# Column sums of the adjacency: from reductions on VectorE to accumulating transfers on GpSimd's queue

## The chip, the cores and the metric

The kernel runs on one core of a Trainium2 chip. The metric is the device time of one launch in microseconds (us), lower is better. The engines are named as in the profile: PE is TensorE (PEld its weight loads), DVE is VectorE, ACT is ScalarE, POOL is GpSimd, SP is SyncE. SP and POOL here only issue transfers; "SPq" is SP's queue.

## The reference, cut to what matters

`x` is [3327, 256] and `adj` is [3327, 3327], all float32. Two graph layers follow each other. The first one needs, beside the row sums of the adjacency, its column sums:

```python
S = S + jnp.eye(n)
Rf = S / jnp.clip(S.sum(axis=1, keepdims=True), 1e-12)
Rb = S / jnp.clip(S.sum(axis=0), 1e-12)[:, None]      # column sums
for s in range(2):                                    # STEPS
    A = _adj_from_feats(Xa, W1, W2, W3)               # softmax over the nucleus (0.9) of each row's logits
    Xf, Xb, Xa = Rf @ Xf, Rb @ Xb, A @ Xa
    Z = Z + (Xf @ U1[s] + Xb @ U2[s] + Xa @ U3[s])
```

The column sums are first used after step one (s = 0), when its products are scaled. The second layer is a masked attention, which the change doesn't touch.

## The kernel before, in words

The 3327 nodes are padded to 3328 = 26 tiles (`T`) of `P` = 128 rows. `step(0)` ("step one", from about 72 us to 1103 us of the span) runs 26 tiles; `between` multiplies by the weights; `step(1)` repeats the work for step two; then comes the second layer. In each step every engine has its own instruction stream, written out by hand, and semaphores order them. The names in the trace carry `s_` for tensors of a step.

A tile t of step one goes through these stages, which are spread over the engines and over three tiles in time:

- PE `make_logits` (L916) computes the tile's 7 chunks of logits into two banks in turn, ACT `store_logits` (L1043) copies each out of its bank.
- DVE `row_max` (L1235) takes the maximum of the row and sends `max_ready` (L1241). ACT `exponentials` (L1050) waits for it, and then runs `guess` and two `probe`s (L1083, L1087, and small instructions to L1101), which end with `searched_early`.
- DVE `start_search` (L1273) waits for `searched_early`; `bisect` runs three times (L1315, late = 3), `threshold` (L1357 to L1383) finds the limit and sends `tau_ready`, `count_needed` (L1388 to L1405) follows.
- ACT `count_ties` (L1128, waits for `tau_ready`) and `lift` (L1134); DVE `settle` (L1410 on) and `keep` (L1428), which sends `kept_ready`.
- PE `turn` (L942) transposes the kept weights, ACT copies them (L1150), PE `multiply` (L952) multiplies; ACT `read_attended` (L1163) and SP store the result.

Beside this, PE `spread` (L928) multiplies each tile of the adjacency. SP's `load_half` (L856) fetches tile t in two halves of [128, 1664] into `adj`; there are NA = 2 pairs of buffers, so tile t+2 is loaded when tile t is used up. `sum_columns(t, h)` (L1433) on DVE also reads each half: it adds up 13 groups of 128 elements into `col_part`. At the end of the step one more DVE reduction (L1525) adds the 26 tiles' parts into `col_inv`.

The order of DVE's stream for tile t is: start_search(t), bisect(t, 0), settle(t-1), row_max(t+1), keep(t-1), bisect(t, 1), bisect(t, 2), sum_columns(t, 0), threshold(t), sum_columns(t, 1), count_needed(t). That of ACT is: store_logits(t+1) chunks 0 and 1, count_ties(t-1), store_logits(t+1) the rest, lift(t-1), exponentials(t+1), guess(t+1), the copies of tile t-1 among the two probes of t+1, read_attended(t-1).

Of the kernel before, what the change touches and what calls it, by code (L numbers as in the profile page):

```python
# [9 lines left out]
ALU = mybir.AluOpType  # L10
ACT = mybir.ActivationFunctionType
AX = mybir.AxisListType

P = 128
# [530 lines left out]
def program(nc, s, x, adjb, adjr, ident_d, W1, W2, W3, U1, U2, U3, gamma, beta, Wks, Wqs, Wvs, WvT, Wo, out):  # L545
    N, T, NP, D, DA, KT = s.N, s.T, s.NP, s.D, s.DA, s.KT
# [10 lines left out]
    with whole, ctx:  # L557
# [206 lines left out]
        def step(number, both):  # L764
# [3 lines left out]
            with ExitStack() as c:  # L768
                def sbt(name, shape, dt=F32):
                    return c.enter_context(nc.sbuf_tensor(tag + name, shape, dt))  # L770

                if first_step:
                    width = SW
                    col_part = sbt("col_part", [P, T, T])
                    spread_out = [sbt(f"spread_out{i}", [P, SW]) for i in range(2)]
                    att_out = [sbt(f"att_out{i}", [P, D]) for i in range(2)]
                else:
                    width = 2 * D
                    z_row = [sbt(f"z_row{i}", [P, D]) for i in range(4)]
                    fold = sbt("fold", [P, DA])  # L780
                    key_sum = sbt("key_sum", [P, 1])
# [41 lines left out]
                         "turned_stored", "attended_groups", "spread_read", "att_read", "setup", "constants_set", "dve",  # L823
                         "act", "low_ready"]
                if first_step:
                    names += ["adj2_loaded", "adj3_loaded", "adj_summed", "spread_stored0", "spread_stored1",
                              "att_stored0", "att_stored1"]
                else:
                    names += ["adj_checked", "guessed", "keys_summed", "keys_folded", "keys_ready", "z_added"]
                    names += [f"z_loaded{i}" for i in range(4)] + [f"z_stored{i}" for i in range(4)]  # L830
# [10 lines left out]
                def half(t, h):  # L841
                    return adj[t % NA * 2 + h][:, :]

                def half_loaded(eng, t, h):
                    eng.wait_ge(sem[f"adj{t % NA * 2 + h}_loaded"], 16 * (t // NA + 1))

                @block.sync
                def _(sp):
                    def load_half(t, h):
                        if t >= NA:  # L850
                            sp.wait_ge(sem[f"adj{h}_used"], t - NA + 1)
                            if first_step:
                                sp.wait_ge(sem["adj_summed"], 2 * (t - NA) + h + 1)
                            else:
                                sp.wait_ge(sem["adj_checked"], 2 * (t - NA) + h + 1)
                        sp.dma_start(half(t, h), adjb[t, :, h * HALF * P:(h + 1) * HALF * P]  # L856
                                     ).then_inc(sem[f"adj{t % NA * 2 + h}_loaded"], 16)

                    def load_z(t):
                        sp.dma_start(z_row[t % 4][:, :], z_d[t, :, :]).then_inc(sem[f"z_loaded{t % 4}"], 16)  # L860

                    def store_z(t):
                        sp.wait_ge(sem["z_added"], t + 1)
                        sp.dma_start(z_d[t, :, :], z_row[t % 4][:, :]).then_inc(sem[f"z_stored{t % 4}"], 16)

                    def store_attended(t):
                        sp.wait_ge(sem["att_read"], t + 1)
                        sp.dma_start(attended_d[t, :, :], att_out[t % 2][:, :]
                                     ).then_inc(sem[f"att_stored{t % 2}"], 16)

                    for t in range(NA):
                        load_half(t, 0)
                        load_half(t, 1)
                    if not first_step:
                        load_z(0)
                        load_z(1)
                    for t in range(T):
                        if not first_step and t > 1:
                            store_z(t - 2)
                        if not first_step and t + 2 < T:  # L880
                            if t >= 2:
                                sp.wait_ge(sem[f"z_stored{(t + 2) % 4}"], 16 * ((t + 2) // 4))
                            load_z(t + 2)
                        if t + NA < T:
                            load_half(t + NA, 0)
                        if first_step:
                            sp.wait_ge(sem["spread_read"], t + 1)
                            sp.dma_start(spread_d[t, :, :], spread_out[t % 2][:, :]
                                         ).then_inc(sem[f"spread_stored{t % 2}"], 16)
                        if t + NA < T:  # L890
                            load_half(t + NA, 1)
                        if first_step and t > 0:
                            store_attended(t - 1)
                    if first_step:
                        store_attended(T - 1)
                        for i in range(2):
                            sp.wait_ge(sem[f"spread_stored{i}"], 16 * (T // 2))
                            sp.wait_ge(sem[f"att_stored{i}"], 16 * (T // 2))
                    else:
                        store_z(T - 2)  # L900
                        store_z(T - 1)
                        for i in range(4):
                            sp.wait_ge(sem[f"z_stored{i}"], 16 * ((T - i + 3) // 4))
# [125 lines left out]
                def _(act):  # L1029
# [145 lines left out]
                    for t in range(T + 1):  # L1175
# [33 lines left out]
                        else:  # L1209
# [16 lines left out]
                            else:  # L1226
                                turned(3, 4, 5, 6)

                @block.vector
                def _(dve):  # L1230
                    chain = Steps(dve, sem["dve"])
# [196 lines left out]
                        dve.scalar_tensor_tensor(kept, kept, col(t, "sharetau"), expd[t % NE][:, :],  # L1428
                                                 ALU.add, ALU.min).then_inc(sem["kept_ready"], 1)

                    def sum_columns(t, h):
                        half_loaded(dve, t, h)
                        dve.tensor_reduce(col_part[:, t, h * HALF:(h + 1) * HALF],  # L1433
                                          half(t, h).rearrange("q (j r) -> q j r", r=P), AX.X, ALU.add
                                          ).then_inc(sem["adj_summed"], 1)

                    def add_spread(t):
                        z = z_row[t % 4][:, :]
                        dve.wait_ge(sem[f"z_loaded{t % 4}"], 16 * (t // 4 + 1))
# [40 lines left out]
                    for t in range(T):  # L1480
                        following, previous = t + 1 < T, t > 0
                        start_search(t)
                        if first_step:
                            bisect(t, 0)
                            if previous:
                                settle(t - 1)
                            if following:
                                row_max(t + 1)
                            if previous:
                                keep(t - 1)  # L1490
                            for k in range(1, late):
                                bisect(t, k)
                            sum_columns(t, 0)
                            threshold(t)
                            sum_columns(t, 1)
                            count_needed(t)
                        else:
                            if previous:
                                settle(t - 1)
                            bisect(t, 0)  # L1500
                            if previous:
                                add_spread(t - 1)
                                keep(t - 1)
                            bisect(t, 1)
                            if following:
                                row_max(t + 1)
                            if t > 1:
                                add_attended(t - 2)
                            bisect(t, 2)
                            if following:  # L1510
                                guess(t + 1)
                            for k in range(3, late):
                                bisect(t, k)
                            threshold(t)
                            count_needed(t)
# [5 lines left out]
                    if not first_step:  # L1521
                        add_attended(T - 1)
                    if first_step:
                        dve.wait_ge(sem["adj_summed"], 2 * T)
                        chain.did(dve.tensor_reduce(col_inv[:, :], col_part[:, :, :].rearrange("q t j -> q j t"),  # L1525
                                                    AX.X, ALU.add))
                        chain.wait()
                        chain.did(dve.tensor_scalar(col_inv[:, :], col_inv[:, :], 1.0, 1e-12, ALU.add, ALU.max))
                        chain.wait()
                        chain.did(dve.reciprocal(col_inv[:, :], col_inv[:, :]))  # L1530
                        chain.wait()
# [257 lines left out]
```

## Time and profile before

| | us |
|---|---|
| median of 3 runs (2746.53 to 2748.87) | 2747.1 |
| the profiled execution, its time | 2744.11 |
| its span, first to last instruction | 2742.1 |
| DVE busy | 2326.4 |
| PE busy | 2266.8 |
| ACT busy | 1911.6 |
| POOL busy | 0.2 |

The difference between the profiled execution's time and its span, 2.0 us, is what lies around the instructions. Busy shares are averages over stages that have different limits; for a change in one stage the rows of that stage are read.

### The profile page before, as it was taken

To read this page: it belongs to the slowest core of one execution; us is meant where nothing else is said; L and a number is where in the kernel's file an instruction comes from. 1 tells how busy PE (TensorE), PEld (TensorE's weight loads), DVE (VectorE), ACT (ScalarE), POOL (GpSimd) and SP (SyncE) were. 2 spreads that over 40 slices of the span, in tenths; PEclk is the share of its full clock that TensorE was granted. 3 is DMA by queue.
4 is the path that set the end of the run, shared out by engine and by line. 5 is a ranking of instruction groups with operands and counts; after the bars stand their busy time and mean duration, and the time that the engine had idled before them with its cause. 6 is when DMAs were issued, how large, how long until landed. Compare 5 with 4: busy or idle time off the path is not lost. (4 is left out here: it accounts for less than half of the span.)

```text
span 2742.1 us, 25827 instructions
## 1 busy us (share of the span) xinstructions
PE 2266.8 (83%) x8302; PEld 1449.3 (53%) x8302; DVE 2326.4 (85%) x4827; ACT 1911.6 (70%) x2579; POOL 0.2 (0%) x4
## 2 busy tenths in 40 slices
PE   5588888888888887899489889898898988989736
PEld 2366666666666666444145545455454554545425
DVE  3499999999999998344699999999999999999825
ACT  3788898888898885233767767677676776767313
POOL 0000000000000000000000000000000000000000
PEclk9699999999999998998689999999999999999868
DMA  1111111111111110311001111111111111111031
GB/s 54 64 45 56 58 58 44 58 44 58 58 57 44 52 51 7 104 58 60 27 25 46 42 33 45 38 46 42 35 40 41 46 42 33 44 40 44 17 122 50
DMA packets 63309, 132.06 MB, mean 48 GB/s; under 512 B 10306, under 2 KB 49857, under 8 KB 63169
## 3 DMA queue, kind: packets, MB, share of 16 engines
q1 hardware_dynamic: 60704, 128.76, 14.9%
q10 hardware_dynamic: 2464, 1.61, 0.2%
q8 instruction: 67, 1.10, 0.2%
q14 instruction: 74, 0.60, 0.1%
HBM read 113.29 MB, written 17.05 MB: 48 GB/s over the span
## 5 line engine op out<-in xcount | busy, mean ns | idle before, releaser
L1315 DVE SCALAR_TENSOR_TENSOR s_junk<-s_logits,s_small,s_expd 128x3327 uint8<-128x3327 f32 x208 | 766.2, 3684 | 7.2
L928 PE MATMUL bank<-both,s_adj 128*128 128x512 f32 x1352 | 646.0, 629 | 0.0
L952 PE MATMUL bank<-h_aug,s_attT 128*128 128x256 f32 x2704 | 626.6, 380 | 20.3 <-ACT s_attT L1150 20.3
L952 PEld LDWEIGHTS bank<-h_aug,s_attT 128*128 128x128 f32 x2704 | 501.9, 190 | 126.4 <-issue 35.9
L928 PEld LDWEIGHTS bank<-both,s_adj 128*128 128x128 f32 x1352 | 270.1, 205 | 294.8 <-issue 292.0
L916 PE MATMUL bank<-KTr,QT 64*128 64x512 f32 (+1 forms) x728 | 275.7, 646 | 142.0 <-ACT s_logits L1043 141.3
L942 PE MATMUL bank<-ident,s_logits 128*128 128x128 f32 x1352 | 216.8, 303 | 194.7 <-DVE s_logits L1428 194.7
L1150 ACT ACTIVATE s_attT<-bank 128x512 f32<-128x512 f32 (+1 forms) x364 | 193.7, 563 | 204.8 <-PE bank L942 182.2
L928 PE MATMUL bank<-h_aug,s_adj 128*128 128x257 f32 x1352 | 333.6, 398 | 2.9 <-ACT s_spread_out L1157 2.9
L1083 ACT ACTIVATE s_junk<-s_expd,s_small 128x3327 int8<-128x3327 f32 x104 | 319.1, 3069 | 1.8
L1087 ACT ACTIVATE s_junk<-s_expd,s_small 128x3327 int8<-128x3327 f32 x104 | 319.4, 3072 | 1.0
L942 PEld LDWEIGHTS bank<-ident,s_logits 128*128 128x128 f32 x1352 | 180.9, 157 | 257.4 <-DVE s_logits L1428 215.9
L928 PEld LDWEIGHTS bank<-h_aug,s_adj 128*128 128x128 f32 x1352 | 257.5, 197 | 86.5 <-issue 47.7
L1050 ACT ACTIVATE s_expd<-s_logits,s_small 128x3327 f32<-128x3327 f32 x52 | 159.6, 3070 | 160.5 <-DVE s_small L1241 86.7
L1043 ACT ACTIVATE s_logits<-bank 128x512 f32<-128x512 f32 (+1 forms) x364 | 188.9, 564 | 99.8 <-PE bank L916 99.7
L916 PEld LDWEIGHTS bank<-KTr,QT 64*128 64x128 f32 x728 | 97.7, 194 | 293.7 <-ACT s_logits L1043 274.8
L1364 DVE MAX8 s_small<-s_logits 128x8 f32<-128x416 f32 (+1 forms) x416 | 209.9, 577 | 0.0
L1235 DVE TENSOR_REDUCE s_small<-s_logits 128x1 f32<-128x3327 f32 x52 | 188.2, 3619 | 24.0 <-ACT s_logits L1043 22.2
L1428 DVE SCALAR_TENSOR_TENSOR s_logits<-s_logits,s_small,s_expd 128x3328 f32<-128x3328 f32 x52 | 191.2, 3676 | 1.9 <-ACT s_logits L1134 1.9
L1357 DVE SCALAR_TENSOR_TENSOR s_logits<-s_logits,s_small,s_expd 128x3327 f32<-128x3327 f32 x52 | 191.3, 3679 | 0.9
L1128 ACT ACTIVATE s_junk<-s_logits,s_small 128x3327 int8<-128x3327 f32 x52 | 159.7, 3072 | 43.6 <-DVE s_small L1383 43.6
L1134 ACT ACTIVATE s_logits<-s_expd,s_small 128x3327 f32<-128x3327 f32 x52 | 159.3, 3064 | 0.9
(213 smaller groups left out, 1878.1 us busy)
## 6 DMA issues: line engine op xcount, KB each, us to landing
s_adj<-adj_turned SPq DMA_DIRECT2D x104, 832.0 KB, 4.6
spread<-s_spread_out SPq DMA_DIRECT2D x26, 128.5 KB, 5.0
m_spread_in<-spread SPq DMA_DIRECT2D x26, 128.5 KB, 2.2
attended<-s_att_out SPq DMA_DIRECT2D x26, 128.0 KB, 4.6
m_att_in<-attended SPq DMA_DIRECT2D x26, 128.0 KB, 2.2
z<-m_z_out SPq DMA_DIRECT2D x26, 128.0 KB, 1.7
s_z_row<-z SPq DMA_DIRECT2D x26, 128.0 KB, 2.0
z<-s_z_row SPq DMA_DIRECT2D x26, 128.0 KB, 1.7
```

Of the source, the lines that this page charges most:

```text
L916: pe.matmul(LB[i % 2][:, 0:w], QT[r:r + DA, bass.ts(t, P)], keys_of(n, w), start=True, stop=True).then_inc(sem["logits_done"], 1)
L928: done = pe.matmul(SX[:, 0:width], half(t, h)[:, bass.ts(jj, P)], rows_of(j), start=(j == 0), stop=(j == T - 1))
L942: last = pe.transpose(TB[i % 4][:, bass.ts(b, P)], kept[:, bass.ts(g + b, P)], ident[:, :])
L952: last = pe.matmul(AB[:, 0:D], attT[i % 4][:, b, :], h_aug[:, g + b, 0:D], start=(g + b == 0), stop=(g + b == T - 1))
L1043: act.activation(logits[t % 3][:, at:at + w], LB[i % 2][:, 0:w], ACT.Copy).then_inc(sem["logits_stored"], 1)
L1083: chain.did(act.activation(junk2[:, 0:N], e, ACT.Relu, bias=at, scale=-0.5, accum_out=col(t, "tail")))
L1087: chain.did(act.activation(junk2[:, 0:N], e, ACT.Sign, bias=at, scale=-0.5, accum_out=col(t, "side")))
L1150: act.activation(attT[i % 4][:, 0:w, :], TB[i % 4][:, 0:w * P].rearrange("q (b r) -> q b r", r=P), ACT.Relu).then_inc(sem["turned_stored"], 1)
L1315: chain.did(dve.scalar_tensor_tensor(junk[:, 0:N], logits[t % 3][:, 0:N], col(t, "cand"), expd[t % NE][:, 0:N], ALU.is_gt, ALU.mult, accum ...
L1357: chain.did(dve.scalar_tensor_tensor(me[:, 0:N], logits[t % 3][:, 0:N], col(t, "cand"), expd[t % NE][:, 0:N], ALU.is_le, ALU.mult, accum_o ...
L1364: chain.did(dve.max(winners(t)[:, 8 * n:8 * n + 8], me[:, at:min(at + NP // SEGMENTS, N)]))
L1428: dve.scalar_tensor_tensor(kept, kept, col(t, "sharetau"), expd[t % NE][:, :], ALU.add, ALU.min).then_inc(sem["kept_ready"], 1)
```

## The change

`sum_columns` and its `col_part` are gone. POOL gets a stream of its own in step one: for each tile it issues two transfers of [128, 1664] from `adjb` (named `adj_turned` in the trace, the same array that SP loads) into a new array `adj_total` (two halves). The first pair overwrites, the other 25 pairs add to what is there (`accum_op`). Before each pair POOL waits for the pair before it. At the end DVE waits for all 52 transfers and reduces `adj_total` to `col_inv`, in two instructions of 13 groups each. SP's loads of step one no longer wait for the sums.

```diff
-                    col_part = sbt("col_part", [P, T, T])
+                    adj_total = [sbt(f"adj_total{i}", [P, HALF * P]) for i in range(2)]
...
                         if t >= NA:
                             sp.wait_ge(sem[f"adj{h}_used"], t - NA + 1)
-                            if first_step:
-                                sp.wait_ge(sem["adj_summed"], 2 * (t - NA) + h + 1)
-                            else:
+                            if not first_step:
                                 sp.wait_ge(sem["adj_checked"], 2 * (t - NA) + h + 1)
...
+                @block.gpsimd
+                def _(pool):
+                    def add_adjacency(t):
+                        if t > 0:
+                            pool.wait_ge(sem["adj_added"], 32 * t)
+                        for h in range(2):
+                            part = adjb[t, :, h * HALF * P:(h + 1) * HALF * P]
+                            if t == 0:
+                                pool.dma_start(adj_total[h][:, :], part).then_inc(sem["adj_added"], 16)
+                            else:
+                                pool.dma_start(adj_total[h][:, :], part, accum_op=ALU.add).then_inc(sem["adj_added"], 16)
+
+                    if first_step:
+                        for t in range(T):
+                            add_adjacency(t)
...
-                    def sum_columns(t, h):
-                        half_loaded(dve, t, h)
-                        dve.tensor_reduce(col_part[:, t, h * HALF:(h + 1) * HALF],
-                                          half(t, h).rearrange("q (j r) -> q j r", r=P), AX.X, ALU.add
-                                          ).then_inc(sem["adj_summed"], 1)
...
-                            sum_columns(t, 0)
                             threshold(t)
-                            sum_columns(t, 1)
                             count_needed(t)
...
-                        dve.wait_ge(sem["adj_summed"], 2 * T)
-                        chain.did(dve.tensor_reduce(col_inv[:, :], col_part[:, :, :].rearrange("q t j -> q j t"),
-                                                    AX.X, ALU.add))
+                        dve.wait_ge(sem["adj_added"], 32 * T)
+                        for h in range(2):
+                            chain.did(dve.tensor_reduce(col_inv[:, h * HALF:(h + 1) * HALF],
+                                                        adj_total[h][:, :].rearrange("q (j r) -> q j r", r=P),
+                                                        AX.X, ALU.add))
```

The first place is DVE's stream in step one, at tile t = 1: the end of bisect(1, 2), threshold(1) and the start of count_needed(1). Before:

```order
L1346 TENSOR_SCALAR s0_small1<-s0_small1 128x1
L1349 SCALAR_TENSOR_TENSOR s0_small1<-s0_small1 128x1
L1433 TENSOR_REDUCE s0_col_part<-s0_adj2 128x13
L1357 SCALAR_TENSOR_TENSOR s0_logits1,s0_small1<-s0_logits1,s0_small1,s0_expd1 128x3327
L1361 TENSOR_TENSOR s0_small1<-s0_small1 128x1
L1364 MAX s0_small1<-s0_logits1 128x8 x8
```

The same place of the change (line numbers are 14 higher):

```order
L1360 TENSOR_SCALAR s0_small1<-s0_small1 128x1
L1363 SCALAR_TENSOR_TENSOR s0_small1<-s0_small1 128x1
L1371 SCALAR_TENSOR_TENSOR s0_logits1,s0_small1<-s0_logits1,s0_small1,s0_expd1 128x3327
L1375 TENSOR_TENSOR s0_small1<-s0_small1 128x1
L1378 MAX s0_small1<-s0_logits1 128x8 x8
```

The reduction of the adjacency half stood ahead of threshold's first pass, and is gone; the second one stood between L1383 and L1388 and is gone in the same way. All else keeps its order.

The second place is POOL's queue in step one, which had nothing before. It begins so (`s_adj_total` is the new array):

```order
L1235 DMA s_adj_total<-adj_turned 128x1664 x2
L1237 DMA s_adj_total<-adj_turned 128x1664 [waits s0_adj_added]
L1237 DMA s_adj_total<-adj_turned 128x1664
L1237 DMA s_adj_total<-adj_turned 128x1664 [waits s0_adj_added]
L1237 DMA s_adj_total<-adj_turned 128x1664
```

26 pairs follow each other, each behind the landing of the one before, and with no wait on any other engine.

The third place is the end of DVE's stream in step one. Before:

```order
L1422 RECIPROCAL s_small<-s_small 128x1 [waits s0_dve]
L1428 SCALAR_TENSOR_TENSOR s_logits<-s_logits,s_small,s_expd 128x3328 [waits s0_lifted,s0_dve]
L1525 TENSOR_REDUCE col_inv<-s_col_part 128x26 [waits s0_adj_summed]
L1528 TENSOR_SCALAR col_inv<-col_inv 128x26 [waits s0_dve]
L1530 RECIPROCAL col_inv<-col_inv 128x26 [waits s0_dve]
```

And of the change:

```order
L1436 RECIPROCAL s_small<-s_small 128x1 [waits s0_dve]
L1442 SCALAR_TENSOR_TENSOR s_logits<-s_logits,s_small,s_expd 128x3328 [waits s0_lifted,s0_dve]
L1532 TENSOR_REDUCE col_inv<-s_adj_total 128x13 [waits s0_adj_added]
L1532 TENSOR_REDUCE col_inv<-s_adj_total 128x13
L1536 TENSOR_SCALAR col_inv<-col_inv 128x26 [waits s0_dve]
L1538 RECIPROCAL col_inv<-col_inv 128x26 [waits s0_dve]
```

The last reduction now waits for the last pair of transfers, and there are two of it.

## Rows read from the trace of the kernel before

**Rows 1.** The page: span, and busy time by engine.

```profile
span 2742.1 us, 25827 instructions
PE 2266.8 (83%) x8302; PEld 1449.3 (53%) x8302; DVE 2326.4 (85%) x4827; ACT 1911.6 (70%) x2579; POOL 0.2 (0%) x4
```

**Rows 2.** A window in step one: us, busy by engine, clock share, DMA share, GB/s.

```profile
400.00:600.00 200.00, 170.12 (x758) 127.37 (x758) 193.22 (x349) 174.33 (x237) 0.00 (x0) 0.98 0.18 55
```

**Rows 3.** Timeline of DVE: start us, us, line, operation; one tile.

```profile
487.11 3.62 DVE L1235 TENSOR_REDUCE s_small<-s_logits 128x1 f32<-128x3327 f32 x1
...
502.94 1.89 DVE L1433 TENSOR_REDUCE s_col_part<-s_adj 128x13 f32<-128x1664 f32 x1
504.74 3.67 DVE L1357 SCALAR_TENSOR_TENSOR s_logits<-s_logits,s_small,s_expd 128x3327 f32<-128x3327 f32 x1
...
515.33 1.88 DVE L1433 TENSOR_REDUCE s_col_part<-s_adj 128x13 f32<-128x1664 f32 x1
...
518.72 0.15 DVE L1273 TENSOR_SCALAR s_small<-s_small 128x1 f32<-128x1 f32 x1
...
524.73 3.62 DVE L1235 TENSOR_REDUCE s_small<-s_logits 128x1 f32<-128x3327 f32 x1
```

**Rows 4.** The column sums on DVE in all of step one.

```profile
L1433 DVE TENSOR_REDUCE s_col_part<-s_adj x52: 1874/1882/1890, 126.5 to 1076.1; 128x13 f32<-128x1664 f32 x52
```

**Rows 5.** Timeline of ACT, the same tile; idle before and its releaser in brackets.

```profile
490.95 3.07 ACT L1050 ACTIVATE s_expd<-s_logits,s_small 128x3327 f32<-128x3327 f32 x1 [3.35 <-DVE s_small L1241]
...
514.04 0.39 ACT L1101 ACTIVATE s_small<-s_small 128x1 f32<-128x1 f32 x1
...
521.89 0.39 ACT L1043 ACTIVATE s_logits<-bank 128x256 f32<-128x256 f32 x1 [0.30 <-PE bank L916]
522.17 3.06 ACT L1134 ACTIVATE s_logits<-s_expd,s_small 128x3327 f32<-128x3327 f32 x1
```

**Rows 6.** Timeline of PE, the same tile.

```profile
511.15 1.13 PE L916 MATMUL bank<-KTr,QT 64*128 64x512 f32 x4
...
521.79 7.22 PE L928 MATMUL bank<-h_aug,s_adj 128*128 128x257 f32 x32
532.19 1.53 PE L942 MATMUL bank<-ident,s_logits 128*128 128x128 f32 x12 [3.18 <-DVE s_logits L1428]
```

**Rows 7.** Timeline of DVE: the row maxima of tiles 2 and 25.

```profile
148.25 3.62 DVE L1235 TENSOR_REDUCE s_small<-s_logits 128x1 f32<-128x3327 f32 x1
...
1013.96 3.62 DVE L1235 TENSOR_REDUCE s_small<-s_logits 128x1 f32<-128x3327 f32 x1
```

**Rows 8.** Timeline of ACT: the last logits of tile 2 copied.

```profile
147.63 0.38 ACT L1043 ACTIVATE s_logits<-bank 128x256 f32<-128x256 f32 x1 [0.30 <-PE bank L916]
```

**Rows 9.** Timeline of DVE, then ACT: the end of step one.

```profile
1076.10 1.88 DVE L1433 TENSOR_REDUCE s_col_part<-s_adj 128x13 f32<-128x1664 f32 x1
...
1082.58 3.68 DVE L1428 SCALAR_TENSOR_TENSOR s_logits<-s_logits,s_small,s_expd 128x3328 f32<-128x3328 f32 x1 [1.85 <-ACT s_logits L1134]
1086.18 1.44 DVE L1525 TENSOR_REDUCE col_inv<-s_col_part 128x26 f32<-128x676 f32 x1
...
1102.77 0.47 ACT L1163 ACTIVATE s_att_out<-bank,s_small 128x256 f32<-128x256 f32 x1 [3.94 <-PE bank L952]
```

**Rows 10.** Transfers of step one: issues, KB each, median us to landing.

```profile
s_adj<-adj_turned SPq DMA_DIRECT2D x52, 832.0 KB, 4.6
spread<-s_spread_out SPq DMA_DIRECT2D x26, 128.5 KB, 5.0
```

**Rows 11.** Timeline of SP's queue: first loads of step one; a tile's first half.

```profile
72.48 56.27 SPq L856 DMA_DIRECT2D s_adj<-adj_turned  x5
...
504.92 0.33 SPq L856 DMA_DIRECT2D s_adj<-adj_turned  x1
```

**Rows 12.** Timeline of PE: the start of step one; the first use of that half.

```profile
105.08 2.56 PE L916 MATMUL bank<-KTr,QT 64*128 64x512 f32 x4 [18.71 <-ACT s_logits L1043]
...
549.83 2.01 PE L928 MATMUL bank<-h_aug,s_adj 128*128 128x257 f32 x8
```

More of the change, by code:

```diff
@@ L825, in step @@
                 if first_step:
-                    names += ["adj2_loaded", "adj3_loaded", "adj_summed", "spread_stored0", "spread_stored1",
+                    names += ["adj2_loaded", "adj3_loaded", "adj_added", "spread_stored0", "spread_stored1",
                               "att_stored0", "att_stored1"]
```

## The prediction

> **What bounds the kernel now.** The page first: DVE is busy for 2326.4 of 2742.1 us, more than PE and ACT [rows 1]. That is a mean over stages, so the windows inside step one come next: of 200 us DVE works 193.22, ACT 174.33, PE 170.12, and the transfer engines are busy for 0.18 of the time [rows 2]. So DVE bounds step one. The timeline of one tile gives the size: from one row maximum to the next (L1235, 487.11 to 524.73) it is 37.62 us, with no idle time shown ahead of any of DVE's instructions [rows 3]. Then I asked how near the others are. ACT has one long wait in a tile, 3.35 us for DVE's maximum (L1050) [rows 5]; PE waits 3.18 us for DVE's `keep` (L942) [rows 6]. Both are waits for DVE; they shrink when DVE gets faster, and how far is what decides here.
>
> **What the change removes.** 52 reductions L1433 of 1.88 us [rows 4]. They overlap the instruction behind them a little: the first one of a tile starts at 502.94 and the next instruction at 504.74 [rows 3], which is 1.80; the second one is as long. So a tile has 3.60 us less of DVE's stream, and DVE alone would need 37.62 - 3.60 = 34.02 us.
>
> **What then is late.** Follow the longest loop that DVE's sums are not part of. Call R the start of a row maximum. ACT's exponentials (L1050) start at R + 3.84 (490.95 - 487.11). From there ACT runs without another long wait to the end of the next tile's last logits copy, at 521.89 + 0.39 = 522.28, which is 31.33 us later [rows 3, 5]. The small waits inside are for PE's banks, which PE in turn gets back from ACT; they belong to the loop. The row maximum of the next tile needs that copy. The hand-over I put at 0.10: between L1235's end (490.73) and L1050's start (490.95) lie 0.22 us, with one small instruction and one hand-over in them. The loop is 3.84 + 31.33 + 0.10 = 35.27 us. It is longer than DVE's 34.02, so the period becomes 35.27, and a tile gains 2.35 us, not 3.60. DVE then waits 1.2 us ahead of L1235 in every tile.
>
> I went through the other waits with R as the origin. `searched_early` is there at 514.04 + 0.39, R + 27.3; DVE asks for it at 518.72 - 487.11 - 3.60 = R + 28.0 (no wait, 0.7 us to spare) [rows 3, 5]. `lift` ends at 522.17 + 3.06 = 525.23; `keep` would start at 522.38 + 3.7 = 526.1 (0.9 to spare) [rows 5]. PE ends its spread at 521.79 + 7.22 = 529.01, R + 41.9, and `keep`, which ends two instructions of 3.7 us behind the start of a row maximum, is ready at R + 35.27 + 7.4 = R + 42.7 (0.8 to spare); its next logits start at 511.15, ACT copies them after 514.43 [rows 5, 6]. Nothing else ends later than the ACT loop, but all margins are under 1 us.
>
> **The sum.** Tile 2 is the first with the full pattern: its maximum starts at 148.25, its logits are there at 148.01, so it can start at 148.11 [rows 7, 8]: 0.14 us. To the maximum of tile 25 at 1013.96 it is 865.7 us for 23 periods; 23 x 35.27 = 811.2, so 54.5. After it there is no further row maximum: DVE's last stretch loses both sums of tile 24 (3.60) and the first of tile 25 (1.80). The second one of tile 25 lies behind `tau_ready`, and DVE waited for ACT's lift there anyway (1.85 us) [rows 9]: nothing. Together 0.1 + 54.5 + 5.4 = 60.0 us.
>
> The new last reductions are two like L1433, 2 x 1.8 us for 1.44 before. Behind `keep` PE and ACT work until 1102.77 + 0.47 = 1103.24, 17 us after L1525 began [rows 9]; the reductions end 13 us before that. Cost nothing; if that cover were gone, 2.2 us.
>
> SP's loads lose a wait. They were not late: a half issued at 504.92 lands in 4.6 us and is first read at 549.83, 45 us after issue [rows 10 to 12]. Gain nothing.
>
> **What it adds: 52 accumulating transfers.** No row of before shows one. A round is the pair of a tile, 2 x 0.85 MB, each round behind the landing of the last. From below: a plain load of the same shape lands in 4.6 us [rows 10], so a pair takes at least that. From above, the slowest transfers of the step: 128.5 KB in 5.0 us [rows 10], which at that rate is 65 us for 1664 KB. An accumulate reads two places and writes one and is otherwise nearest in shape to the plain load (same source, same 128 rows of 1664 floats), so I take two reads in turn for each half: 4 x 4.6 = 18 us for a pair. Then 26 rounds end at about 72 + 26 x 18 = 540 us, in the middle of step one, and DVE's last wait is over long before.
>
> The point from which it counts: step one would end at 1103.2 - 60 = 1043.2; DVE needs some 4.2 us behind the last landing (3.6 for the two reductions and 0.6, an estimate, for the small ones behind), and the first load of the step is issued at 72.48 [rows 11]. So rounds may take (1043.2 - 4.2 - 72.5) / 26 = 37.2 us before they cost anything, and at (1103.2 - 4.2 - 72.5) / 26 = 39.5 us the whole gain is used up. 37 us is twice my estimate and eight times the lower bound.
>
> A rule beside it: the Trainium skill (Collectives: The Full Stack, The bandwidth ceiling) holds that adding on the way costs nothing by itself, and that a reducing transfer runs at half the rate of a copy, since each piece needs two source reads. No row of before can show that. By it a pair takes 9 to 18 us, and the sum stays the same.
>
> The new transfers share the transfer engines with SP's. These are busy for 0.18 now [rows 2]. If the accumulates fill them, a load takes three times as long, 14 us, against 45 us of room. At the start of the step ACT holds PE for 18.71 us [rows 12], so late first halves cost nothing either.
>
> **The rivals.**
>
> *A. The transfers are too slow* (the other side). One mechanism: the chain of 26 rounds, not DVE, ends step one, and DVE waits at L1532 of the changed kernel. The step ends at 72.5 + 26r + 4.2 us for a round of r. At r = 50 this is 1376.7 against 1103.2, and the kernel takes 2747.1 + 273.5 = 3021; at the upper bound of 65 it is 3411. For it: nothing in the trace bounds such a transfer, and each round waits for the last to land. Against it: it needs a rate of under 1.70 MB / 39.5 us = 43 GB/s where the mean of step one is already 55 with engines busy for 0.18. It decides from 39.5 us.
>
> *B. GpSimd's transfers disturb DVE.* POOL's preparation of a transfer and DVE's instructions may hold each other up. For it: POOL did nothing before, so no row excludes it. With rounds of 18 us and tiles of 35, four issues fall on each of the first 13 tiles. If each held DVE by one of its long instructions, 3.67 us [rows 3], 13 x (14.7 - 1.2) = 175 us would be lost, 1.2 being DVE's room: 2862, a slower kernel. At a quarter of that length it is 13 x (3.7 - 1.2) = 32: 2719.
>
> The Trainium skill has a rule of this kind (SBUF — State Buffer, the section on two separate sides): while DVE runs a copy-like instruction in its two-port mode, GpSimd cannot write its descriptors, and its transfer waits. By it the chain suffers, not DVE. DVE's long instructions of step one are reductions, maxima and two-input ones, which that page of the Trainium skill does not count among these, so it would change little; a hold-up of 3.7 us for each of 52 issues would make my round 25 us, still under 37.
>
> *C. The gain is that of DVE in full.* If ACT's loop gave way too, the period is 34.02: 23 x 3.62 + 5.4 = 88 us, 2659. Against it: the loop's instructions are untouched, and its end at 522.28 is only 2.4 us ahead of the maximum that needs it.
>
> *D. The waits of under 1 us add up.* Each margin that fails adds to a period; with 0.5 us it is 23 x 0.5 = 11 us less: 2698.
>
> **How the numbers follow.** The profiled execution's 2744.1 becomes 2684; the median of the runs lies 3.0 above it, so I predict 2747.1 - 60 = 2687 for the median. Main case (period of 35.0 to 35.8, with D's inner half): 2680 to 2699, chance 0.72. B with a loss of up to 50: 0.08. C: 0.04. Rounds between 37.2 us and the point of no gain: 0.02, half of it within 0.2%. A: 0.13, B with more than 60: 0.01. The range takes in the main case, most of B and part of the way to C: 2670 to 2715; the slower cases (0.14) and C stay outside. A measurement of this kernel tells 0.2%, 5.5 us, from no change. Faster: 0.72 + 0.08 + 0.04 + 0.01 = 0.85; same 0.01; slower 0.14.
>
> **What would show it.** Right: the distance of two L1249 (the row maximum in the changed kernel) is 35.3 us, with a wait of about 1.2 us ahead of it for ACT's L1041; the wait of ACT's L1048 for the maximum shrinks from 3.35 to about 1.0; the last accumulate lands near 540 us, and L1532 waits for nothing. Wrong: a period of 37.6 with waits of DVE elsewhere (D), longer DVE instructions while POOL issues (B), a period of 34.0 (C), or a wait of DVE for a transfer ahead of L1532 (A), which would be the costliest.

## The result, and the profile after

The changed kernel takes 2687.11 us (median of 4 runs, 2686.05 to 2688.84); the kernel before, timed on the same chip, 2746.82. The ratio is 0.9782, with a 95% interval of 0.9765 to 0.9799: 59.7 us less, where 60 were forecast. The profiled execution of the changed kernel took 2686.23 us.

The page of the changed kernel, where [rows 1] stand for the kernel before:

```profile
span 2684.4 us, 25754 instructions
PE 2245.3 (84%) x8302; PEld 1431.1 (53%) x8302; DVE 2235.7 (83%) x4776; ACT 1909.5 (71%) x2579; POOL 45.2 (2%) x56
```

DVE lost 2326.4 - 2235.7 = 90.7 us of work, the kernel 57.7 us of span. The difference is what this case is about. The timeline of DVE in the changed kernel, from one row maximum to the next (L1249 is L1235 of before), shows where it is:

```profile
500.76 3.62 DVE L1249 TENSOR_REDUCE s_small<-s_logits 128x1 f32<-128x3327 f32 x1 [1.24 <-ACT s_logits L1041]
...
516.60 3.68 DVE L1371 SCALAR_TENSOR_TENSOR s_logits<-s_logits,s_small,s_expd 128x3327 f32<-128x3327 f32 x1
...
528.80 0.15 DVE L1287 TENSOR_SCALAR s_small<-s_small 128x1 f32<-128x1 f32 x1
...
536.03 3.62 DVE L1249 TENSOR_REDUCE s_small<-s_logits 128x1 f32<-128x3327 f32 x1 [1.24 <-ACT s_logits L1041]
```

The period is 536.03 - 500.76 = 35.27 us, against 37.62 in [rows 3], and a wait of 1.24 us stands ahead of each row maximum, where there was none. It ends when ACT has copied the last logits. ACT's side in the same tile, and PE's:

```profile
500.28 0.38 ACT L1041 ACTIVATE s_logits<-bank 128x256 f32<-128x256 f32 x1 [0.30 <-PE bank L914]
...
504.61 3.07 ACT L1048 ACTIVATE s_expd<-s_logits,s_small 128x3327 f32<-128x3327 f32 x1 [0.99 <-DVE s_small L1255]
```

```profile
508.22 1.53 PE L940 MATMUL bank<-ident,s_logits 128*128 128x128 f32 x12 [0.82 <-DVE s_logits L1442]
```

ACT's wait for the maximum fell from 3.35 us [rows 5] to 0.99, PE's for `keep` from 3.18 [rows 6] to 0.82: both by 2.36, about what the period fell by. The ends of the stretch answer to [rows 7]:

```profile
148.17 3.62 DVE L1249 TENSOR_REDUCE s_small<-s_logits 128x1 f32<-128x3327 f32 x1 [3.38 <-ACT s_logits L1041]
...
959.13 3.62 DVE L1249 TENSOR_REDUCE s_small<-s_logits 128x1 f32<-128x3327 f32 x1 [1.25 <-ACT s_logits L1041]
```

(959.13 - 148.17) / 23 = 35.26 us a tile. The last maximum starts 54.8 us earlier than before. The end of step one, as in [rows 9]:

```profile
1019.28 0.16 DVE L1424 TENSOR_TENSOR s_small<-s_small 128x1 f32<-128x1 f32 x1 [1.82 <-ACT s_junk L1126]
1022.38 3.68 DVE L1442 SCALAR_TENSOR_TENSOR s_logits<-s_logits,s_small,s_expd 128x3328 f32<-128x3328 f32 x1 [1.85 <-ACT s_logits L1132]
1025.98 3.67 DVE L1532 TENSOR_REDUCE col_inv<-s_adj_total 128x13 f32<-128x1664 f32 x2
```

The last `keep` starts at 1022.38 instead of 1082.58, 60.2 us earlier. The second sum of the last tile was forecast to bring nothing; the new wait of 1.82 us (L1424, for ACT's tie count) is where it went. L1532 waits for nothing.

The transfers. POOL's timeline, start and end of the chain of 26 pairs, and the list of issues from 72 to 1110 us (KB each, median us to landing):

```profile
73.15 1.25 POOL L1235 DMA_DIRECT2D s_adj_total<-adj_turned  x2 [72.70 <-POOLq L592]
87.62 1.78 POOL L1237 DMA_DIRECT2D s_adj_total<-adj_turned  x2 [13.22 <-DMA s_adj_total<-adj_turned]
99.13 1.73 POOL L1237 DMA_DIRECT2D s_adj_total<-adj_turned  x2 [9.73 <-DMA s_adj_total<-adj_turned]
...
382.14 1.75 POOL L1237 DMA_DIRECT2D s_adj_total<-adj_turned  x2 [10.31 <-DMA s_adj_total<-adj_turned]
```

```profile
s_adj<-adj_turned SPq DMA_DIRECT2D x52, 832.0 KB, 5.6
s_adj_total<-adj_turned POOLq DMA_DIRECT2D x52, 832.0 KB, 10.3
```

A round takes (382.14 - 73.15) / 25 = 12.4 us, so the chain is over at about 395 us, 630 us before DVE asks for it (L1532 at 1025.98).

### The profile page after: what moved, and what is told of

Same layout as the page of the kernel before. It is cut to its first block and busy times, and to the rows that moved or that the text cites. A ratio compares the mean times of both kernels' runs of the same rounds, so it can differ in the third digit from the quotient of the medians.

```text
span 2684.4 us, 25754 instructions
## 1 busy us (share of the span) xinstructions
PE 2245.3 (84%) x8302; PEld 1431.1 (53%) x8302; DVE 2235.7 (83%) x4776; ACT 1909.5 (71%) x2579; POOL 45.2 (2%) x56
## 3 DMA queue, kind: packets, MB, share of 16 engines
q0 software_dynamic: 7488, 44.31, 8.5%
## 5 line engine op out<-in xcount | busy, mean ns | idle before, releaser
L1329 DVE SCALAR_TENSOR_TENSOR s_junk<-s_logits,s_small,s_expd 128x3327 uint8<-128x3327 f32 x208 | 766.2, 3684 | 7.2
L940 PE MATMUL bank<-ident,s_logits 128*128 128x128 f32 x1352 | 202.7, 289 | 147.1 <-DVE s_logits L1442 147.1
L926 PE MATMUL bank<-h_aug,s_adj 128*128 128x257 f32 x1352 | 323.4, 390 | 2.9 <-ACT s_spread_out L1155 2.9
L926 PEld LDWEIGHTS bank<-h_aug,s_adj 128*128 128x128 f32 x1352 | 251.4, 192 | 84.8 <-issue 47.7
L940 PEld LDWEIGHTS bank<-ident,s_logits 128*128 128x128 f32 x1352 | 168.0, 148 | 208.1 <-DVE s_logits L1442 168.3
L1048 ACT ACTIVATE s_expd<-s_logits,s_small 128x3327 f32<-128x3327 f32 x52 | 159.7, 3071 | 115.0 <-issue 73.7
L1249 DVE TENSOR_REDUCE s_small<-s_logits 128x1 f32<-128x3327 f32 x52 | 188.2, 3619 | 54.8 <-ACT s_logits L1041 53.9
L1371 DVE SCALAR_TENSOR_TENSOR s_logits<-s_logits,s_small,s_expd 128x3327 f32<-128x3327 f32 x52 | 191.6, 3684 | 1.9
L1132 ACT ACTIVATE s_logits<-s_expd,s_small 128x3327 f32<-128x3327 f32 x52 | 159.3, 3064 | 0.9
## 6 DMA issues: line engine op xcount, KB each, us to landing
s_adj_total<-adj_turned POOLq DMA_DIRECT2D x52, 832.0 KB, 10.3
```

The lines of the kernel that those rows point to most:

```text
L926: done = pe.matmul(SX[:, 0:width], half(t, h)[:, bass.ts(jj, P)], rows_of(j), start=(j == 0), stop=(j == T - 1))
L940: last = pe.transpose(TB[i % 4][:, bass.ts(b, P)], kept[:, bass.ts(g + b, P)], ident[:, :])
L1329: chain.did(dve.scalar_tensor_tensor(junk[:, 0:N], logits[t % 3][:, 0:N], col(t, "cand"), expd[t % NE][:, 0:N], ALU.is_gt, ALU.mult, accum ...
L1371: chain.did(dve.scalar_tensor_tensor(me[:, 0:N], logits[t % 3][:, 0:N], col(t, "cand"), expd[t % NE][:, 0:N], ALU.is_le, ALU.mult, accum_o ...
```

## The experiments

Each kernel is the changed kernel with one edit, where nothing else is said; times are medians, and the ratios are to the kernel before, timed on the same chip. The experiments were timed in three other sets than the result, and the kernel before came to 2748.0 to 2749.1 us there instead of 2746.8; so a difference of 2 us to the changed kernel's 2687.11 means nothing by itself. Experiments 1, 3, 5 and 6 are one set, 2, 4, 8 and 9 another, 7, 10 and 11 the third. The periods read from the traces decide the small differences. Two theories stood against each other. **Theory:** when DVE's sums go, a loop through ACT and the row maximum, 35.27 us long, sets the period. **Rivals:** the transfers or their traffic hold back the rest of DVE's gain; or DVE's own stream still sets the time.

**1. No transfers.**

```diff
-                    if first_step:
-                        for t in range(T):
-                            add_adjacency(t)
+                    if False:
+                        add_adjacency(0)
...
-                        dve.wait_ge(sem["adj_added"], 32 * T)
                         for h in range(2):
+                            half_loaded(dve, T - 1, h)
...
-                                                        adj_total[h][:, :].rearrange("q (j r) -> q j r", r=P),
+                                                        half(T - 1, h).rearrange("q (j r) -> q j r", r=P),
```

> The changed kernel without its 52 transfers; the column sums are left out (those of the last tile alone stand in for them). Theory (ACT's loop of 35.27 us a tile sets the period): the transfers cost nothing, so 2687, within 2 us of the changed kernel, and still 1.2 us of wait ahead of each row maximum. Rival (the transfers or their traffic on the transfer engines keep DVE from its full gain): period 34.02 us, 2659.

Measured: 2687.0 us (2686.63 to 2689.81), the same as with them. The row maxima (L1248 there) still wait:

```profile
501.02 3.62 DVE L1248 TENSOR_REDUCE s_small<-s_logits 128x1 f32<-128x3327 f32 x1 [1.26 <-ACT s_logits L1041]
536.32 3.62 DVE L1248 TENSOR_REDUCE s_small<-s_logits 128x1 f32<-128x3327 f32 x1 [1.26 <-ACT s_logits L1041]
```

From the maximum of tile 2 to that of tile 25 a tile takes 35.29 us here, (959.73 - 148.16) / 23, against 35.26 with the transfers. They cost nothing, and what DVE's gain lacks is not theirs.

**2. The kernel before, with the transfers added.** It keeps its sums on DVE and gets POOL's chain beside them, which DVE also awaits at the end. Cut to the lines that issue and await the pairs; `add_adjacency` and `adj_total` are as in the change.

```diff
...
+                    if first_step:
+                        for t in range(T):
+                            add_adjacency(t)
...
                         dve.wait_ge(sem["adj_summed"], 2 * T)
+                        dve.wait_ge(sem["adj_added"], 32 * T)
```

> The kernel before with its sums on DVE, and the 52 accumulating transfers added to it (their result is unused). Here DVE sets the period of 37.62 us without any room. Theory: the transfers disturb no engine, 2747, within 3 us of the kernel before, and DVE's long instructions keep 3.68 us while the transfers run. Rival (POOL's issues hold DVE up): 52 issues each cost up to 3.7 us of a DVE that has no room, 2800 or more; at a quarter of that 2795.

Measured: 2748.63 us, ratio 1.0000 (0.9991 to 1.001). In the groups of DVE, first from 105 to 380 us with the chain under way, then from 500 to 1000 us without it, the longest two-input form takes the same 3684 ns:

```profile
L1332 DVE SCALAR_TENSOR_TENSOR s_junk<-s_logits,s_small,s_expd 128x3327 uint8<-128x3327 f32 x22 | 81.1, 3684 | 0.5
...
L1332 DVE SCALAR_TENSOR_TENSOR s_junk<-s_logits,s_small,s_expd 128x3327 uint8<-128x3327 f32 x40 | 147.4, 3684 | 1.0
```

A tile takes 37.65 us from the maximum of tile 3 to that of tile 24, (978.10 - 187.41) / 21, against 37.64 in the kernel before. So POOL's issues hold DVE up by nothing that can be seen, here where DVE has no room to hide it. The rival's full price would have been 52 x 3.7 = 192 us, 2939, and not only the 2800 that was written down; the measurement excludes the quarter of it too.

**3. ACT's loop 0.36 us shorter.** The copy of the attended rows moves into a wait of ACT for PE's bank, one tile later.

```diff
                             if following:
-                                store_logits(t + 1, range(2, NC))
+                                store_logits(t + 1, (2, 3))
+                            if t > 1:
+                                read_attended(t - 2)
+                            if following:
+                                store_logits(t + 1, range(4, NC))
...
-                            if previous:
-                                read_attended(t - 1)
+                            if t == T:
+                                read_attended(T - 1)
```

> The changed kernel with ACT's copy of the attended rows (L1161, 0.45 us long, 0.36 us of ACT's stream) moved out of the stretch between the last probe and the first logits copies, to stand one tile later between logits chunks 3 and 4, where ACT waits 0.73 us for PE. Theory (ACT's loop): the period falls from 35.27 to 34.91 us, 23 x 0.36 = 8 us less, 2679. Rival (DVE or the transfers set the period): no change, 2687.

Measured: 2679.21 us, 7.9 less than the changed kernel and 7.8 less than experiment 1, which ran beside it. ACT's timeline there:

```profile
494.22 1.08 ACT L1041 ACTIVATE s_logits<-bank 128x512 f32<-128x512 f32 x2
495.18 0.49 ACT L1161 ACTIVATE s_att_out<-bank,s_small 128x256 f32<-128x256 f32 x1
496.02 1.09 ACT L1041 ACTIVATE s_logits<-bank 128x512 f32<-128x512 f32 x2 [0.36 <-PE bank L914]
...
501.74 3.07 ACT L1048 ACTIVATE s_expd<-s_logits,s_small 128x3327 f32<-128x3327 f32 x1 [0.99 <-DVE s_small L1259]
...
536.65 3.07 ACT L1048 ACTIVATE s_expd<-s_logits,s_small 128x3327 f32<-128x3327 f32 x1 [0.99 <-DVE s_small L1259]
```

The copy fills half of the bank's wait (0.36 us are left of 0.73), and the period is 34.91 us here, 0.36 less; from tile 2 to tile 25 the mean is 34.92, (951.85 - 148.68) / 23, against 35.26.

**4. The same move in the kernel before.**

> The kernel before with the same move of ACT's copy of the attended rows as in the run on the changed kernel. Theory: DVE sets the period here, ACT waits 3.35 us a tile for it, so the move only lengthens that wait: 2747, no change. Rival (the move is worth its 8 us wherever it is made): 2739.

Measured: 2749.34 us, ratio 1.0004 (0.9994 to 1.0013). The same edit is worth 8 us in the changed kernel and nothing in the kernel before: there DVE set the period, and after the change ACT's loop does. From 105 to 1060 us ACT's waits for PE's banks (L1043) fell from 32.8 us in all to 24.8, and its waits for the maximum rose from 73.0 to 76.6. So the move only exchanged waits; less than half of the 8.0 us shows ahead of the maximum, where all of it was expected.

**5. and 6. DVE's stream made longer again.** One more reduction a tile, of 832 or 1664 columns.

```diff
+                            chain.did(dve.tensor_reduce(pair(t, "width", 0), expd[t % NE][:, 0:832], AX.X, ALU.add))
                             threshold(t)
```

> The changed kernel with one more DVE reduction a tile, of 832 columns of the exponentials, ahead of the threshold pass (its result is unused); about 0.9 us. Theory: DVE's own stream grows from 34.02 to 34.9 us, still under ACT's loop of 35.27, so the period stays, and only the last two tiles show it: 2687 to 2689. Rival (DVE's stream still sets the time): 25 x 0.9 = 22 us more, 2709.

> The same with 1664 columns, 1.8 us, as long as one column sum of before. Theory: DVE's stream is 35.82 us, 0.55 above ACT's loop; 23 x 0.55 = 12.7 plus 2 x 1.8 at the end, 16 us more: 2703. Rival (DVE's stream still sets the time): 25 x 1.8 = 45 us more, 2732.

Measured: 2692.92 and 2708.6 us, 5.8 and 21.5 us more than the changed kernel. Both lie nearer to the theory (0 to 2, and 16) than to the rival (22 and 45), and both are some 4 to 6 us above the theory. The row maxima of the 832-column kernel show a detail that neither foresaw:

```profile
467.75 3.62 DVE L1249 TENSOR_REDUCE s_small<-s_logits 128x1 f32<-128x3327 f32 x1 [0.34 <-ACT s_logits L1041]
503.38 3.62 DVE L1249 TENSOR_REDUCE s_small<-s_logits 128x1 f32<-128x3327 f32 x1 [0.68 <-ACT s_logits L1041]
538.67 3.62 DVE L1249 TENSOR_REDUCE s_small<-s_logits 128x1 f32<-128x3327 f32 x1 [0.34 <-ACT s_logits L1041]
```

Periods of 35.63 and 35.29 us alternate; ahead of the longer one, ACT's copy was over at 502.93 and the row maximum began only 0.45 us later, where 0.10 is usual. In the 1664-column kernel too every second maximum starts late, by 0.26 us:

```profile
473.57 3.62 DVE L1249 TENSOR_REDUCE s_small<-s_logits 128x1 f32<-128x3327 f32 x1
509.65 3.62 DVE L1249 TENSOR_REDUCE s_small<-s_logits 128x1 f32<-128x3327 f32 x1 [0.26 <-DVE s_small L1436]
545.51 3.62 DVE L1249 TENSOR_REDUCE s_small<-s_logits 128x1 f32<-128x3327 f32 x1
```

The late starts account for most of what lies above the theory in the first of the two. From the maximum of tile 2 to that of tile 25 a tile takes 35.45 us there, (964.22 - 148.79) / 23, instead of 35.26: 4.5 of the 5.8 us, which leaves 1.3 for the ends of the step, as forecast. With 1664 columns it is 35.96, (977.11 - 149.94) / 23, which gives 16.2 us where 12.7 were forecast.

**7. Two reductions of 416 columns instead of one of 832.**

> The changed kernel with two added DVE reductions a tile, of 416 columns each, in place of the one of 832 that took 6 us instead of 0 to 2; there every second row maximum started 0.35 us late though its logits were there. If that delay goes with the number of instructions in a tile's stream, it is gone here and the time is 2687 to 2690. If it goes with DVE's small room of about 0.3 us, it stays: 2692 or more.

Measured: 2689.8 us. DVE's room, 0.26 us, is smaller than the 0.34 with the single reduction, yet the late starts are gone:

```profile
501.57 3.62 DVE L1249 TENSOR_REDUCE s_small<-s_logits 128x1 f32<-128x3327 f32 x1 [0.26 <-ACT s_logits L1041]
536.82 3.62 DVE L1249 TENSOR_REDUCE s_small<-s_logits 128x1 f32<-128x3327 f32 x1 [0.26 <-ACT s_logits L1041]
572.09 3.62 DVE L1249 TENSOR_REDUCE s_small<-s_logits 128x1 f32<-128x3327 f32 x1 [0.25 <-ACT s_logits L1041]
```

So about 1 us of extra DVE work a tile is free once nothing delays its start, as the theory says, and the late start doesn't go with the room. It goes with something else in which the two kernels differ: the number of instructions in a tile's stream, or their place or length. These are not told apart, and the cause stays open.

**8. Plain transfers in place of the accumulating ones.**

```diff
-                                pool.dma_start(adj_total[h][:, :], part, accum_op=ALU.add).then_inc(sem["adj_added"], 16)
+                                pool.dma_start(adj_total[h][:, :], part).then_inc(sem["adj_added"], 16)
```

> The changed kernel with plain transfers in place of the accumulating ones on GpSimd's queue; the column sums are then those of the last tile alone. Nothing depends on their length, so 2687. A pair of accumulating ones took 12.4 us (25 pairs from 73.2 to 382.7). If the second read costs as much as the first, a plain pair takes about half the moving time, some 7 us, so that the last pair is issued near 72 + 25 x 7 = 250 us; if adding costs nothing it takes 12 us again and the last pair is issued near 380.

Measured: 2686.22 us (one run). The last pair is issued at:

```profile
279.79 1.05 POOL L1237 DMA_DIRECT2D s_adj_total<-adj_turned  x2 [5.88 <-DMA s_adj_total<-adj_turned]
```

With the first at 73.06 a round is 8.3 us against 12.4: adding makes a pair 1.5 times as long, neither twice nor the same. In the pages' lists of queues the same 7488 packets take 4.6% of 16 engines' span plain and 8.5% accumulating, 1.85 times as much. Why the whole pair grows by less was not measured; that a part of it (the issue, the wait for the landing) does not double is the likely reason. One half lands in a median of 6.3 us in step one, against 10.3 accumulating. The issue itself is longer too, 1.75 us a pair against 1.05.

**9. The chain four times as long,** 104 pairs.

> The changed kernel with the 26 pairs made four times over, 104 pairs in a chain (the column sums come out four times too large). Theory (the chain of transfers costs nothing until it outlasts step one, and then all of the excess): 104 x 12.4 = 1290 us, the step ends at 73 + 1290 + 4 = 1367 against 1043, 324 us more: 3011; tiles of step one still take 35.27 us. If the transfers slow the loads or the engines, the tiles get longer too and it is more.

Measured: 2980.62 us (one run), 293.5 more than the changed kernel, and DVE at the end of step one:

```profile
1022.95 3.68 DVE L1442 SCALAR_TENSOR_TENSOR s_logits<-s_logits,s_small,s_expd 128x3328 f32<-128x3328 f32 x1 [1.85 <-ACT s_logits L1132]
1333.96 3.68 DVE L1532 TENSOR_REDUCE col_inv<-s_adj_total 128x13 f32<-128x1664 f32 x2 [307.33 <-DMA s_adj_total<-adj_turned]
```

The work on the tiles ends when it did (1022.95 against 1022.38), with the transfer engines busy for 0.88 to 0.90 of the time; SP's loads took 6.8 us to land instead of 5.6, without effect. Then DVE waits for 307 us. This is rival A of the prediction, made to happen: it costs the whole excess of the chain over the step, and nothing before. The forecast of 324 was 30 too high since a round is 12.1 us in this run, (1333.96 - 73) / 104; it falls to 11.4 when no loads run beside it.

**10. and 11. A shorter loop.** If the loop through the row maximum is the limit, it can be cut at the maximum itself: its first part needs only the chunks that are there already. In the second kernel the edit of experiment 3 is added.

```diff
+                        if first_step:
+                            dve.wait_ge(sem["logits_stored"], (t + 1) * NC - 2)
+                            chain.did(dve.tensor_reduce(pair(t, "width", 0), logits[t % 3][:, 0:2560], AX.X, ALU.max))
+                            dve.wait_ge(sem["logits_stored"], (t + 1) * NC)
+                            chain.did(dve.tensor_reduce(pair(t, "width", 1), logits[t % 3][:, 2560:N], AX.X, ALU.max))
+                            chain.wait()
+                            dve.tensor_scalar(col(t, "negmax"), pair(t, "width", 0), pair(t, "width", 1), -1.0,
+                                              ALU.max, ALU.mult).then_inc(sem["max_ready"], 1)
+                            chain.did(dve.tensor_tensor(col(t, "max"), pair(t, "width", 0), pair(t, "width", 1),
+                                                        ALU.max))
```

> The changed kernel with DVE's row maximum of step one in two parts: the first 2560 columns (chunks 0 to 4) as soon as they are copied, the last 767 when the rest is. Both parts together take some 0.3 us more than one. Theory (the loop through ACT and the row maximum sets 35.27): only the second part, about 1 us, is then in the loop, ACT's wait of 0.99 us goes, and the bound is DVE's stream of 34.02 + 0.3 to 0.4 or ACT's of 34.28, so about 34.4; 23 x 0.87 = 20 us less, 2667. Rival (DVE's or ACT's own stream is already the limit, with waits that only move): 0.3 us more a tile, 2694.

> The split row maximum and the later copy of the attended rows together. Theory: ACT's stream falls to 33.9 us, but DVE's 34.3 to 34.4 is then the longer one, so it is the same as with the split alone, 2665 to 2667, and not 8 us faster.

Measured: 2665.13 us (ratio to the kernel before 0.9697, 0.9684 to 0.9711) and 2660.92 (0.9682, 0.9668 to 0.9695), the fastest version of this study, 26 us under the changed kernel. DVE's timeline in the second:

```profile
487.14 2.82 DVE L1254 TENSOR_REDUCE s_small<-s_logits 128x1 f32<-128x2560 f32 x1
489.88 0.94 DVE L1256 TENSOR_REDUCE s_small<-s_logits 128x1 f32<-128x767 f32 x1
490.86 0.21 DVE L1258 TENSOR_SCALAR s_small<-s_small 128x1 f32<-128x1 f32 x1
...
521.39 2.82 DVE L1254 TENSOR_REDUCE s_small<-s_logits 128x1 f32<-128x2560 f32 x1
```

No wait is left ahead of the maximum, and the period is 34.25 us, DVE's own stream. The split alone left it at 34.44 ((936.35 - 144.29) / 23, between first parts of the maxima of tiles 2 and 25). There ACT's exponentials (L1048) follow `lift` (L1132) without a wait:

```profile
489.60 3.06 ACT L1132 ACTIVATE s_logits<-s_expd,s_small 128x3327 f32<-128x3327 f32 x1
492.60 3.07 ACT L1048 ACTIVATE s_expd<-s_logits,s_small 128x3327 f32<-128x3327 f32 x1
```

So ACT's stream, with its short waits for PE's banks, was the limit; the later copy shortens it by 0.36 us, and DVE's takes over 0.19 further down. I had expected the second edit to bring nothing, since I put DVE's stream at 34.3 to 34.4 and so not below ACT's; it brought 4.2 us.

## Why the prediction was right, point by point

- *DVE bounds step one, and the sums leave 34.02 us of it.* Right: no wait before, and 35.27 - 1.24 = 34.03 after. Experiment 11 confirms it with the waits gone: its 34.25 holds the split, which lengthens DVE's way from the start of the maximum to the start of `keep` from 3.73 us (500.76 to 504.49 in the changed kernel) to 3.92 (487.14 to 491.06), and without these 0.19 it is 34.06.
- *The loop of 35.27 us.* Right to 0.01 us, and shown by experiments 1, 3, 4 and 10: the gap to DVE's full gain isn't the transfers'; 0.36 us out of the loop is 0.34 to 0.36 off the period, but only after the change; and the loop can be cut. The waits forecast (1.2, about 1.0, some 0.8) were measured as 1.24, 0.99 and 0.82. The other waits with under 1 us of room (rival D) did not fail.
- *The sum.* 0.1 + 54.5 + 5.4 was forecast, and 0.1 (148.25 to 148.17), 54.7 and 5.4 (from 54.8 at the last maximum to 60.2 at the last `keep`) were measured. Some 2.5 us of it are missing between the two spans (57.7). They are lost behind step two, which still ends 60.5 us earlier, and it is the kernel before whose profiled execution is unusual: from the first instruction behind step two (L129) to the end of the span it takes 117.7 us, where the changed kernel and all the kernels of the experiments take 120.3 to 120.7, the two built on the kernel before too. That is also why its profiled execution (2744.11) lay 3.0 us under its median, and why the forecast of 2684 for the changed kernel's (2686.23) was 2 us short. The forecast of the median is the median before less 60, so it did not suffer from this.
- *The transfers.* The path was right, the size off: a round was put at 18 us and measured at 12.4. The term that was mis-sized is "two reads in turn for each half: 4 x 4.6". A plain pair on this queue takes 8.3 us, under 2 x 4.6: its halves land in a median of 6.3 us each (experiment 8), so they overlap. And adding makes the pair 1.5 times as long, not twice. Nothing hung on it, with a bound of 37.2 us. The Trainium skill's rule (Collectives: The Full Stack, The bandwidth ceiling) puts a reducing transfer at half the rate of a copy. The time of a packet, 1.85 times that of a plain one, nearly agrees; the time of a whole pair, 1.5 times, doesn't.
- *Rival A,* a chain that outlasts the step: excluded for 26 pairs, shown for 104, with the price of the formula once the round is the measured one.
- *Rival B,* POOL disturbing DVE: excluded by experiment 2. The Trainium skill's rule on GpSimd's transfers beside DVE's two-port instructions (SBUF — State Buffer, the section on two separate sides) would hold up the chain. A round takes 12.4 us beside step one and 11.4 with every engine idle, but in step one the loads run too, and no run tells the two apart. DVE has no long instruction here of the kind that the rule names, so no run tests it.
- *SP's loads.* They took 5.6 us in step one instead of 4.6, not the 14 that I allowed, and no engine's wait for them shows in the trace from 100 to 1043 us.

## What to carry to other kernels

Work taken off the busiest engine is worth only the distance to the next loop. That distance can be read before the change: start at the instruction for which the other engine waits, follow the chain through both engines until it returns to the same instruction of the next tile, and leave out what the change removes. Here the loop came to 35.27 us, and a busy share of 87% for ACT would have suggested more room than there was. Once such a loop is the limit, the place to cut it is the instruction at which it changes engines: reducing what had already arrived ahead of the last piece gave 22 us.

A chain of transfers with nothing else waiting for it was free here until it outlasted its stage, and then cost all of the excess; so its price is one comparison, round length times rounds against the stage.

## What was not expected of the hardware

- An accumulating transfer of 832 KB (128 rows of 6656 bytes) from memory into the array landed in 10.3 us, two at a time; a pair took 12.4 us beside the loads and 11.4 alone, against 8.3 for a plain pair on the same queue beside the same loads. Its issue kept POOL for about 0.9 us against 0.5.
- With one reduction added to DVE's stream of a tile, every second row maximum began 0.26 to 0.35 us late, without any producer that was late; with two shorter ones added it did not. On 26 tiles this is 3 to 4 us, more than the effect that the experiment was made to measure. The cause is open.
